# Two GpSimd sums of the channel norm, in four instructions of one row each

## The reference, cut to what matters

```python
def _L1_attn_ref(x, w_qkv, b_qkv, w_fc, b_fc, gamma, beta):
    ...
    out = out @ w_fc + b_fc
    out = out + x
    mu = jnp.mean(out, axis=-1, keepdims=True)
    var = jnp.mean(jnp.square(out - mu), axis=-1, keepdims=True)
    out = (out - mu) * jax.lax.rsqrt(var + EPS) * gamma + beta
    return out
...
x = _layernorm(x + _L0_attn_ref(...))
x = _layernorm(x + _L0_ffn_ref(...))
x = _layernorm(x + _L1_attn_ref(...))
x = _layernorm(x + _L1_ffn_ref(...))
```

## Time and profile before

| | us |
|---|---|
| median of 3 runs | 1427.6 (1427.54 to 1428.34) |
| the profiled execution | 1430.41 |
| its span, first to last instruction | 1428.6 |
| TensorE busy in the span | 1372.3 (96%) |
| VectorE busy | 1071.4 (75%) |
| ScalarE busy | 870.2 (61%) |
| GpSimd busy | 258.4 (18%) |

### The profile page before, as it was taken

How to read it: one execution, slowest core, us unless ns; L and a number is a source line. 1 busy time by engine, 2 the same in 40 slices (tenths; PEclk the granted TensorE clock), 3 DMA queues, 4 the chain that set the end, 5 groups by cost and what they waited for, 6 DMA issues and landing times. The chain is left out here.

```text
span 1428.6 us, 44125 instructions
## 1 busy us (share of the span) xinstructions
PE 1372.3 (96%) x18460; PEld 846.4 (59%) x18460; DVE 1071.4 (75%) x2004; ACT 870.2 (61%) x1775; POOL 258.4 (18%) x388
## 2 busy tenths in 40 slices
PE   7999999999999999999999999899987699999998
PEld 4554344444444444444444444788776589999997
DVE  2567888988888888889888880555788576777666
ACT  3445668778787787787877877655455333333342
POOL 4332011102110111021111110000345411111111
PEclk9999999999999999999999999999998599999999
DMA  7685311212212211122300000314424544445441
GB/s 222 212 209 122 73 25 37 46 30 50 48 33 46 45 36 46 31 51 46 93 3 3 3 3 2 118 43 161 172 74 151 201 181 178 175 181 183 167 180 73
DMA packets 77824, 134.08 MB, mean 94 GB/s; under 512 B 12226, under 2 KB 64443, under 8 KB 72252
## 3 DMA queue, kind: packets, MB, share of 16 engines
q1 hardware_dynamic: 59612, 108.84, 25.8%
q10 hardware_dynamic: 14608, 14.00, 3.0%
q0 software_dynamic: 3408, 8.43, 1.7%
HBM read 67.75 MB, written 23.11 MB: 64 GB/s over the span
## 5 line engine op out<-in xcount | busy, mean ns | idle before, releaser
L1799 DVE TENSOR_REDUCE part_max<-pair 128x2 f32<-128x1024 f32 (+2 forms) x576 | 643.2, 1161 | 73.5 <-PE pair L1216 44.4
L1611 ACT ACTIVATE big<-pair 128x512 f32<-128x512 f32 (+1 forms) x1120 | 584.9, 598 | 185.4 <-PE pair L1244 176.2
L1244 PE MATMUL pair<-big 128*32 128x512 bf16 (+3 forms) x5120 | 345.1, 349 | 3.9 <-DMA big<-max_t 3.3
L1216 PE MATMUL pair<-big 128*32 128x512 bf16 (+3 forms) x5120 | 340.7, 349 | 4.9 <-DVE part_max L1799 4.5
L1266 PE MATMUL pair<-big 128*17 128x512 f32 (+3 forms) x2560 | 288.0, 528 | 0.7 <-POOL big L2228 0.3
L1216 PEld LDWEIGHTS pair<-big 128*32 128x32 bf16 x5120 | 125.1, 96 | 185.5 <-DVE part_max L1799 87.1
L1244 PEld LDWEIGHTS pair<-big 128*32 128x32 bf16 x5120 | 123.2, 96 | 158.1 <-ACT big L1611 71.6
L1624 ACT ACTIVATE std<-moments,eps_col 128x1 f32<-128x1 f32 (+1 forms) x110 | 32.5, 295 | 220.8 <-DVE moments L1837 211.3
L1502 PE MATMUL pair<-big,tok 128*128 128x128 f32 x1248 | 148.1, 278 | 7.2 <-DVE big L2112 7.2
L1502 PEld LDWEIGHTS pair<-big,tok 128*128 128x128 f32 x1248 | 147.2, 194 | 10.2 <-DVE big L2112 8.3
L1514 PE MATMUL pair<-big 128*128 x624 | 141.0, 379 | 0.0
(11 more groups left out here) (184 smaller groups left out, 1285.2 us busy)
## 6 DMA issues: line engine op xcount, KB each, us to landing
tok<-big SPq DMA_DIRECT2D x39, 1024.0 KB
big<-in_L_ffn_w SPq DMA_DIRECT2D x16, 1024.0 KB
big<-split_dram SPq DMA_DIRECT2D x216, 64.0 KB, 2.8
split_dram<-big ACTq DMA_DIRECT2D x32, 384.0 KB, 4.0
big<-split_dram SPq DMA_DIRECT2D x42, 256.0 KB, 4.2
big<-routed_dram SPq DMA_DIRECT2D x39, 129.0 KB, 2.1
tok<-in_L_attn_x SPq DMA_DIRECT2D x8, 512.0 KB, 6.7
big<-in_c_query_rows SPq DMA_DIRECT2D x8, 512.0 KB, 4.9
```

Source lines behind the costliest of these rows:

```text
L1216: mm = pe.matmul(bank[q:q + STRIPE, o:o + w], m.q_op[slot][:, step.qt, h, step.r * P + q:step.r * P + q + STRIPE], m.k_op[slot][:, h, step ...
L1244: mm = pe.matmul(m.bank[step.bank][k:k + STRIPE, n * w:(n + 1) * w], m.k_op[slot][:, h, step.kb * P + k:step.kb * P + k + STRIPE], m.q_op[ ...
L1611: act.activation(m.p_ring[:, step.place, step.heads[0]:step.heads[-1] + 1, step.at:step.at + w], m.bank[step.bank][:, 0:len(step.heads) * ...
L1799: dve.tensor_reduce(m.part_max[(step.u * QT + step.qt) % 2][:, step.r, step.heads[0]:step.heads[0] + n, step.c], banks[:, :, 0:w], X, ALU. ...
```

## The change

`ShiftBeta` and `Combine` each issue four instructions of one row of 256 columns in place of one of 1024. Each row signals, so `beta_added` and `combined` count four for each group, and VectorE's two waits for `combined` have their thresholds multiplied by four: `Add` and the F `Moments` still wait for the whole group. In `Combine`, row r waits for row r of the first sum; before, the one instruction waited for the one.

```diff
@@ -1880,7 +1880,7 @@
                 dve.wait_ge(s.bias_in, 16)
                 dve.wait_ge(s.normed, step.normed)
             elif g >= 2:
-                dve.wait_ge(s.combined, g - 1)
+                dve.wait_ge(s.combined, BPT * (g - 1))
             for half, b in enumerate(step.banks):
                 addend = {"O": m.res[g % 2][:, 2 * half:2 * half + 2, :],
                           "S": m.spectral_bias[:, :].unsqueeze(1).broadcast_to([P, 2, D]),
@@ -1899,7 +1899,7 @@
 
         elif isinstance(step, Moments):
             if step.stage == "F":
-                dve.wait_ge(s.combined, step.g + 1)
+                dve.wait_ge(s.combined, BPT * (step.g + 1))
             take_moments(dve, m, s, step.i, m.norm_rows(step.stage, step.g))
 
         elif isinstance(step, Shift):
@@ -2241,13 +2241,16 @@
             pool.wait_ge(s.product, 2 * step.m + 2)
             pool.wait_ge(s.grammed, step.g // TPB + 1)
             pool.wait_ge(s.norm_params_in, 32)
-            pool.tensor_tensor(m.group(step.g), m.group(step.g), m.beta.unsqueeze(1).broadcast_to([P, BPT, D]),
-                               ALU.add).then_inc(s.beta_added, 1)
+            for r in range(BPT):
+                row = m.group(step.g)[:, r, :]
+                pool.tensor_tensor(row, row, m.beta, ALU.add).then_inc(s.beta_added, 1)
 
         elif isinstance(step, Combine):
-            pool.wait_ge(s.beta_added, step.g + 1)
             pool.wait_ge(s.scaled, step.g + 1)
-            pool.tensor_tensor(m.group(step.g), m.group(step.g), m.res[step.g % 2][:, :, :], ALU.add).then_inc(s.combined, 1)
+            for r in range(BPT):
+                row = m.group(step.g)[:, r, :]
+                pool.wait_ge(s.beta_added, BPT * step.g + r + 1)
+                pool.tensor_tensor(row, row, m.res[step.g % 2][:, r, :], ALU.add).then_inc(s.combined, 1)
 
         elif isinstance(step, PadTile):
```

## The result

The changed kernel takes 1424.3 us in the median of 22 runs (1419.3 to 1428.5), the kernel before, timed beside it, 1428.5 (22 runs, 1424.6 to 1432.1). The ratio is 0.9969, 95% interval 0.9960 to 0.9978: 4.2 to 4.4 us, faster by 0.3%. Forecast were 3.5 us and 1424.1.

A forecast was written before the change was run, and what follows sets the result against it. No engine is full in the channel norm's stretch; short waits bound it, VectorE locked out during GpSimd's sums. Terms 0.4 + 1.3 + 0.8 - 0.5 + 1.5 = 3.5 us gave 1424.1 us, range 1421.3 to 1427.9.

The forecast's parts named there:

- the largest term: Channel norm's tail, L2017 at 1102.64: its stall was to shrink from 2.33 to 0.85 us, worth 1.5 us.

The follow-up runs named there:

- the probes: Two programs of their own without the computation: GpSimd bursts beside one VectorE instruction; 4 columns lasted 0.58 us beside rows, 2.18 beside one whole sum.

## What to carry to other kernels

A VectorE instruction of 4 columns that lasts 2 us, and ends when a GpSimd instruction ends, waits for the port; cut GpSimd's instruction at its largest, the one that stands beside the critical small steps (here the second sum, which alone brought as much as both), into pieces of about 0.6 us, and not smaller, since eighths lost the gain again; halves, of 1.2 us, brought none. Expect most waits to shrink to one piece, but not each: a few missed one to six ends here. Where the engine that gains is followed by an idle TensorE, read the granted clock after that idle time: in these traces it was worth as much as the largest term.

## What was not expected of the hardware

- Handing over the lock: in the probes at the next end of a GpSimd instruction in every one of 64 trials; in the full kernel L1898 missed three ends three times out of three, an L1997 of 8 columns six ends of pieces of 128 columns (2.65 us), L1988 and L2017 one of 512. Cut into 256 columns, the same multiply took turns with GpSimd's rows.
- A large VectorE instruction that gets in between rows holds GpSimd in turn: five rows 4.42 us, not 3.44; in the full kernel four rows 3.26, not 2.60.
- Four rows of 256 columns on GpSimd cost 2.60 us, two of 512 in 2.32, eight of 128 in 3.15, one of 1024 in 2.18.
- One kernel's fold took 3.72 us in one execution and 6.74 in another (on two chips), by the granted clock.
- Idle times of 1.4 to 4.8 us on VectorE, once with ScalarE, which the profile puts down to a remote releaser, in four of these twelve traces and not in others of the same kernels; in three of the four they end at the same moment of the span, 1130.8.
